# Two gated attention and feed-forward layers on one core: POOL's list re-ordered around DVE's routing, products without a reader in the filling

## What is computed

```python
x = x + tanh(g_xattn[0]) * attn0(layernorm(x), ctx)    # 16 heads of 8
x = x + tanh(g_ffn[0])   * experts(layernorm(x))       # 16 experts, best 4 of each token
x = x + tanh(g_xattn[1]) * attn1(layernorm(x), ctx)    # one head
x = x + tanh(g_ffn[1])   * butterfly_ffn(layernorm(x))

# experts
logits = xn @ wg + bg
vals, idx = top_k(logits, 4); gates = softmax(vals)    # ties: the lower index first
h = einsum('th,ehd->etd', xn, w1) + b1                 # every expert on every token
s = a * sigmoid(1.702 * a) * (b + 1)                   # a, b: even and odd columns, clipped
t = sum over e of gate_full[t, e] * (s_e @ w2_e + b2_e)

# butterfly_ffn: 9 stages on 512 columns each way, around a gelu
h = butterfly(x @ W_exp + b_exp, up_weights)
h = gelu(h + up_bias)
y = butterfly(h, down_weights) @ W_con + b_con + down_bias
```

## Time and profile before

| | us |
|---|---|
| median of 3 runs | 392.1 |
| lowest, highest | 389.17, 392.59 |
| profiled execution | 395.04 |
| its span, first to last instruction | 393.1 |

### The profile page before, as it was taken

One profiled execution on the slowest core, in us unless ns is written; L12 is line 12 of the kernel. 1 busy time (PEld: TensorE's weight loads), 2 busy tenths in 40 slices (PEclk: granted clock), 3 DMA queues, 4 the chain that ended last, 5 costly groups with the idle time before them and its releaser, 6 DMA issues.

```text
span 393.1 us, 7226 instructions
## 1 busy us (share of the span) xinstructions
PE 324.5 (83%) x2600; PEld 228.2 (58%) x2600; DVE 257.4 (65%) x602; ACT 209.6 (53%) x405; POOL 206.9 (53%) x270
## 2 busy tenths in 40 slices
PE   5758689698799912899199998799998999899986
PEld 2435567576577811666066665566655666555866
DVE  8531436556466287398868789697896887795450
ACT  2642146466366610567145584765866746855543
POOL 7463899979598999999600193002900059122120
PEclk9996759989899755699779999999999999999999
DMA  7669222645531233333133222232322433100001
GB/s 245 129 142 120 86 63 107 133 131 120 112 110 59 69 123 116 128 106 105 29 104 116 80 91 72 85 119 67 105 87 80 119 95 108 53 0 1 28 28 55
DMA packets 17235, 36.66 MB, mean 93 GB/s; under 512 B 2384, under 2 KB 4068, under 8 KB 17064
## 3 DMA queue, kind: packets, MB, share of 16 engines
q1 hardware_dynamic: 13184, 23.53, 21.2%
q0 software_dynamic: 3168, 11.54, 10.8%
q10 hardware_dynamic: 848, 1.14, 0.9%
HBM read 32.79 MB, written 1.18 MB: 86 GB/s over the span
## 4 chain that ended last, share of the span: by engine, by line
PE 36%; POOL 32%; DMA 11%; DVE 7%; issue 6%; ACT 6%; SPq 1%; ACTq 0%; DVEq 0%; POOLq 0%
PE bank L1005 9%; POOL bft L365 6%; POOL bfx L369 5%; POOL bfly L373 5%; PE bank L996 5%; PE bank L994 4%; PE bank L995 4%; DMA bw<-in_L_ffn_w 4%; DMA bw<-in_flies 4%; PE bank L1128 4%; PE bank L1113 3%; DMA x_sb<-in_x 3%; POOL bw L339 2%; POOL w_lo L388 2%; POOL v_all L422 2%
## 5 line engine op out<-in xcount | busy, mean ns | idle before, releaser
L994 PE MATMUL bank<-xhl,w_hi 128*128 128x512 f32 x128 | 76.3, 596 | 0.5 <-ACT rings L734 0.5
L734 ACT ACTIVATE rings<-bank,cols 128x512 f32<-128x512 f32 x64 | 44.1, 689 | 60.9 <-PE bank L996 50.1
L1245 DVE TENSOR_REDUCE nt<-bank 128x4 f32<-128x480 f32 x64 | 39.9, 650 | 46.2 <-PE bank L878 46.2
L1434 DVE SCALAR_TENSOR_TENSOR rings<-rings,gates 128x512 f32<-128x512 f32 x64 | 47.9, 749 | 20.9 <-ACT rings L734 20.5
L996 PE MATMUL bank<-xhl,w_hi 128*128 128x512 f32 x128 | 51.6, 403 | 0.0
L995 PE MATMUL bank<-xhl,w_lo 128*128 128x512 f32 x128 | 51.5, 402 | 0.0
L871 PE MATMUL bank<-rings,ks 32*120 32x128 f32 x512 | 41.7, 306 | 11.4 <-DMA rings<-mxr 6.2
L878 PE MATMUL bank<-ks,rings 32*128 32x120 f32 x512 | 42.9, 312 | 5.8 <-DMA rings<-qt_row 4.0
L871 PEld LDWEIGHTS bank<-rings,ks 32*120 32x120 f32 x512 | 35.2, 201 | 17.4 <-DMA rings<-mxr 8.5
L738 ACT ACTIVATE rings<-bank,b1c 128x512 f32<-128x512 f32 x64 | 44.0, 688 | 1.0 <-PE bank L996 0.6
L878 PEld LDWEIGHTS bank<-ks,rings 32*128 32x128 f32 x512 | 36.5, 213 | 6.6 <-issue 4.2
(11 more groups left out here) (227 smaller groups left out, 688.1 us busy)
## 6 DMA issues: line engine op xcount, KB each, us to landing
gates<-gate_rows SPq DMA_DIRECT2D x64, 256.0 KB, 3.1
bw<-in_flies POOLq DMA_DIRECT2D x18, 512.0 KB, 4.3
bw<-in_L_ffn_w POOLq DMA_DIRECT2D x4, 512.0 KB, 7.8
x_sb<-in_x SPq DMA_DIRECT2D x4, 256.0 KB, 8.3
x_sb<-in_L_ffn_w SPq DMA_DIRECT2D x1, 1024.0 KB, 4.9
wide<-in_ctx ACTq DMA_DIRECT2D x4, 240.0 KB, 7.2
ks<-kt_row SPq DMA_DIRECT2D x16, 60.0 KB
out<-xr SPq DMA_DIRECT2D x3, 256.0 KB, 2.4
```

What stands on the lines that cost most here:

```text
L734: act.activation(esg[:, e % 2, :], SB[1 + e % 2][:, :], ACT.Gelu_apprx_sigmoid, bias=b1_in[:, 0, e:e + 1]).then_inc(s["m_sg"], 1)
L994: pe.matmul(bk[:, :], w1_hi[:, e, branch, :], low(g), start=True, stop=False)
L1245: dve.tensor_reduce(nt[:, b % 2, OF[n], :], score_bank(b, n)[:, 0:HR * M].rearrange("p (r m) -> p r m", r=HR), AX.X, ALU.max, negate=True) ...
L1434: dve.scalar_tensor_tensor(eq[:, j, :], esg[:, j, :], GELU_LIMIT, gates[:, (n - 1) % NG, :], ALU.min, ALU.mult).then_inc(s["m_eq"], 1)
```

## The change

It has four parts.

- **POOL's list.** The seven bias stages move between the second and third split of `w1`. The 18 butterfly stages are spread: 0 to 9, `norm2(0)` and `norm_rows(0)`, 10 and 11, `remainders(0)`, then a wait until DVE has written the gates of group 0, `norm_rows(1)`, 12 and 13. In the first group of experts: the ties of group 1, a wait for its gates, `remainders(1)`, `norm2(1)`, `norm_rows(2)`, stages 14 and 15, the four `values1`. In the second group stage 16, in the third stage 17 and the bias's last stages, each behind a wait for the next group's gates.
- **DVE's list.** The routing of group 0 stands before the residual of sequence 13 as a whole; before, its first part stood ahead of it and the rest behind.
- **ACT's list.** The exponentials of the gates (L664) and the copy of the turned gates (L670) stand before the copy of the heads, not behind the copy of the turned attention.
- **PE's list.** `keep_busy` issues eight products of 128x256 whose result nobody reads, two at each of four places of the filling.

```diff
--- before.py
+++ after.py
@@ -380,7 +380,18 @@
             fetch(1)
             pool.tensor_scalar(b1c[:, :], b1_in[:, 1, :], 1.0, None, ALU.add).then_inc(s["b1_rdy"], 1)
 
+            def up_bias_rows():
+                pool.wait_ge(s["ld_ub"], 16 * 2)
+                for k in range(STAGES - 2):
+                    src, w = ubs[:, k % 2, :], ubw[:, 2 * k * P:2 * (k + 1) * P]
+                    straight(bft[0:HC, 0:P], w[:, 0:P], src)
+                    crossed(ubs[:, 2, :], w[:, P:2 * P], src, 2 ** k, P)
+                    summed(ubs[:, (k + 1) % 2, :], bft[0:HC, 0:P], ubs[:, 2, :])
+                pool.tensor_copy(ubs[:, 2, 0:1], ubs[:, 1, 0:1]).then_inc(s["us_rdy"], 1)
+
             for q in range(NQ):
+                if q == NQ // 2:
+                    up_bias_rows()
                 fetched(q)
                 src = bw[:, q % 2, :].rearrange("p (e t c) -> p e t c", e=4, t=2)
                 hi, lo = w1_hi[:, 4 * q:4 * q + 4, :, :], w1_lo[:, 4 * q:4 * q + 4, :, :]
@@ -397,14 +408,6 @@
                                    bcast[:, BO, :].unsqueeze(1).to_broadcast([P, GB, D]), ALU.add).then_inc(s["xr_rdy"], 1)
             own.then_wait(pool.tensor_tensor(bcd[:, :], bcast[:, BC, :], bcast[:, BD, :], ALU.add))
             own.then_wait(pool.tensor_scalar(bcd[:, :], bcd[:, :], tg[:, 3:4], None, ALU.mult))
-
-            pool.wait_ge(s["ld_ub"], 16 * 2)
-            for k in range(STAGES - 2):
-                src, w = ubs[:, k % 2, :], ubw[:, 2 * k * P:2 * (k + 1) * P]
-                straight(bft[0:HC, 0:P], w[:, 0:P], src)
-                crossed(ubs[:, 2, :], w[:, P:2 * P], src, 2 ** k, P)
-                summed(ubs[:, (k + 1) % 2, :], bft[0:HC, 0:P], ubs[:, 2, :])
-            pool.tensor_copy(ubs[:, 2, 0:1], ubs[:, 1, 0:1]).then_inc(s["us_rdy"], 1)
 
             def up_bias_stages():
                 pool.wait_ge(s["ub_rdy"], 1)
@@ -515,11 +518,21 @@
                 pool.tensor_tensor(rows_, rows_, bcd[:, :].unsqueeze(1).to_broadcast([P, GB, D]), ALU.add
                                    ).then_inc(s["d_bias"], 1)
 
+            def stages(ks_):
+                for k in ks_:
+                    for op in range(3):
+                        stage(k, op)
+
             def mixture(g):
                 if first(g):
                     router_ties(1)
+                    pool.wait_ge(s["m_gf"], 2)
                     remainders(1)
+                    norm2(1)
                     norm_rows(2)
+                    stages(range(STAGES + 5, STAGES + 7))
+                    for i in range(G):
+                        values1(i)
                 else:
                     rows_again(g - 1)
                     if not last(g):
@@ -527,8 +540,15 @@
                     attn1_scales(g - 1)
                     if not last(g):
                         router_ties(g + 1)
+                        pool.wait_ge(s["m_gf"], g + 2)
                     if g + 2 < G:
                         norm_rows(g + 2)
+                    if not last(g):
+                        stages((STAGES + 6 + g,))
+                    if g == G - 2:
+                        pool.tensor_copy(bft[0:1, 0:1], bfly[0:1, STAGES % 2, 0:1]).then_inc(s["bf_rdy"], 1)
+                        pool.wait_ge(s["bf_rdy"], 1)
+                        up_bias_stages()
                     if last(g):
                         pool.wait_ge(s["x3_st"], G - 2)
                         norm_scales(stats[:, 0:2 * GB, :], mean[:, 0:2 * GB], rr[:, 0:1, 0:2 * GB], 2 * GB
@@ -537,21 +557,14 @@
                         with_biases(0)
                         with_biases(1)
 
-            for k in range(2 * STAGES):
-                for op in range(3):
-                    stage(k, op)
-                if k == STAGES:
-                    norm2(0)
-                    norm_rows(0)
-                if k == 2 * STAGES - 3:
-                    remainders(0)
-                    norm_rows(1)
-            pool.tensor_copy(bft[0:1, 0:1], bfly[0:1, STAGES % 2, 0:1]).then_inc(s["bf_rdy"], 1)
-            pool.wait_ge(s["bf_rdy"], 1)
-            up_bias_stages()
-            for g in range(G):
-                values1(g)
-            norm2(1)
+            stages(range(STAGES + 1))
+            norm2(0)
+            norm_rows(0)
+            stages(range(STAGES + 1, STAGES + 3))
+            remainders(0)
+            pool.wait_ge(s["m_gf"], 1)
+            norm_rows(1)
+            stages(range(STAGES + 3, STAGES + 5))
             pipelined(pool, mixture)
             inverse_root(3, GB, False, GB)
             inverse_root(4, GB, False)
@@ -681,16 +694,16 @@
                 if b < NB:
                     exps(b, 0)
                     exps(b, 1)
+                if b == NB - 1:
+                    router_exp(0)
+                if b == NB:
+                    gates_t(0)
                 if 0 <= b - 1 < NB:
                     heads_out(b - 1)
                 if b == NB - 2:
                     normed_t(0)
-                if b == NB:
-                    gates_t(0)
                 if 0 <= b - 2:
                     attn_t(b - 2)
-                if b == NB - 1:
-                    router_exp(0)
                 if b < NB:
                     exps(b, 2)
                     exps(b, 3)
@@ -937,6 +950,12 @@
                     mm = pe.transpose((SB[0] if first(g) else PO)[0:E, u * P:(u + 1) * P], gf[:, u, :], ident[:, :])
                 mm.then_inc(s["m_g_turned"], 1)
 
+            def keep_busy(bk, n):
+
+                for _ in range(n):
+                    pe.matmul(bk[:, 0:2 * P], ident[:, :], wt[:, WK0:WK0 + 2, :].rearrange("p i c -> p (i c)"),
+                              start=True, stop=True)
+
             phase(-2, 0)
             queries(2)
             both_values(3)
@@ -950,13 +969,18 @@
             phase(-1, 0)
             pe.wait_ge(s["v_rdy"], 2 * G)
             turn_max(0)
+            keep_busy(PO, 2)
             phase(-1, 1)
             pe.wait_ge(s["kt_rdy"], G)
             pe.wait_ge(s["bo_rdy"], 1)
             for b in range(NB):
+                if b <= 1:
+                    keep_busy(PO, 2)
                 phase(b, 0)
                 if b + 1 < NB:
                     turn_max(b + 1)
+                if b == 0:
+                    keep_busy(PO, 2)
                 if b == NB - 2:
                     turn_normed(0)
                 if b >= 1:
@@ -1334,12 +1358,12 @@
                         maxima(b + 2, n)
                 if b == NB - 1:
                     router_top(0)
+                    router_ties(0)
+                    router_chosen(0)
+                    router_gates(0)
                 if b >= 2:
                     residual(b - 2)
                 if b == NB - 1:
-                    router_ties(0)
-                    router_chosen(0)
-                    router_gates(0)
                     dve.wait_ge(s["ub_turned"], 1)
                     dve.tensor_copy(ubx[:, 0, :], bank[2][:, 0:HC]).then_inc(s["ub_rdy"], 1)
 
```

## The result

| | us |
|---|---|
| before, measured beside it | 391.06 median of 4 runs (389.17 to 392.59) |
| after | 381.36 median of 4 runs (378.53 to 382.75) |
| ratio | 0.974, 95% interval 0.969 to 0.979 |
| profiled execution of after, its span | 380.01, 377.9 |

Faster by 2.6%, where 5.4% was forecast. The place to read first is the timeline of PE, and in it each group's turned gates (L937 before, L950 now). Columns: start, duration, instruction, and in brackets the idle time ahead of it.

What follows compares the result with a forecast made beforehand. It took PE's two waits for DVE's gates, 23.6 us together, as the bound, with DVE held by POOL. 15.2 + 1.4 + 10.2 - 5.5 + 0 + 0 = 21.3 us off the 392.1 median gave 370.8 us, range 362 to 380.

Steps and rivals of the forecast that it cites:

- The first term: Routing of group 0: undisturbed by POOL, PE's wait for the gates goes, 15.2 us, plus 1.4 from a faster clock.
- The second term: Routing of group 1: PE's wait of 8.3 us and the expert at half clock go, 10.2 us gained.
- The third term: Experts behind the gates of group 1: POOL's work there now comes too late or holds DVE, minus 5.5 us.
- Its first view: Second group: POOL's list brings the rows for DVE's sum 5.1 us late, stopping ACT and PE too.
- Its second view: Same stretch: 15 long POOL instructions hold DVE 16 us; spare time and cover leave a 6 us delay.
- The rest: Second and third group: stages 16 and 17 and routing without POOL's rows ready, taken as 0, between minus 3 and plus 3.
- The products: Filling: eight unread products cost 7.6 us at worst, against an earlier full clock; taken as 0, minus 5 to plus 4.
- B: Rival: stages beside experts cost more, a gain of only 12 us, 380 us; chance 0.17.
- both delays: Experts: late POOL rows and DVE held by POOL add up instead of being one delay, 12 us.
- C: Rival: DVE's small routing instructions are slow for another reason than POOL, so routing only begins earlier, 382 us; chance 0.07.
- A: Rival: POOL's list is not late in the second group, so 26.8 us are gained, 365.3 us; chance 0.17.
- D: Rival: slower, as POOL and DVE wait for each other in turn at DVE's second-group sum; chance 0.04.

Runs made afterwards that it cites:

- e4: The changed kernel without POOL's wait for the gates of group 0: ratio 0.987 to the kernel before, median 388.37 us.
- e5: The changed kernel with POOL's rows for DVE's sum made right behind `norm2(1)`, same work: ratio 0.969 to before, median 379.30 us.
- e10: e2 with the arithmetic of stages 14 and 15 left out, their transfers kept: ratio 0.948 to before, median 370.45 us.
- e9: e2 with a wait that puts stages 16 and 17 behind their group's second attention: ratio 0.965 to before, median 380.91 us.
- e1: The changed kernel without the eight products nobody reads: ratio 0.973 to before, median 382.51 us.
- e11: The kernel before with the eight products nobody reads and nothing else: ratio 1.002 to before, median 392.32 us.
- e2: The changed kernel with the four `values1` moved ahead of the low part of group 0, into the attention: ratio 0.957 to before, median 376.53 us.
- e6: The changed kernel with an always-met wait behind each of the four `values1` instructions: ratio 0.972 to before, median 380.76 us.

## Why the prediction was wrong

The sign and the two places were right, the size not: 370.8 was forecast, 381.4 came, past the upper end of 380.

**The first term, 15.2 plus 1.4.** Right. The wait went from 15.21 to 0.90 us, so 14.3 us, POOL's low part ended at 133.5, and e4 shows the mechanism.

**The second term, 10.2.** Right. Of it 8.3 us lie in front of the second gates and 1.9, the slow expert, behind them. From the first gates to the second it took 41.2 us and takes 31.3, so 9.9 us, where 8.3 and the 1.4 of the first expert were forecast; the second wait is 0.39 us, and POOL idles from 149.4 to 156.1. At the second gates the forecast comes to a lead of 24.9 us, and 26.9 was measured. That excess is luck: 2.7 us of the lead are the clock at the end of the filling.

**The third term, minus 5.5, is the step that failed.** Its first view, POOL's list too late for DVE's sum, described a delay that is not there: the rows were ready 4.5 us before DVE came, and e5 shows that making them 18 us sooner changes nothing. Its second view, DVE held by POOL beside the experts, was the true one, and was priced too low: 16 us of holding, less 6 us of spare time and 4 us of cover. The holding was sized well. In the second group of after eleven of DVE's 128x512 instructions were held, and took 17.7 us longer together than undisturbed (0.42 or 0.69 each). What failed is the 10 us taken off it. In e10 the holding in this group is 5.8 us, so 11.9 less, and the group is 11.9 us shorter (42.6 against 54.4): that part of the holding reached the end in full. Against before the group is 7.9 us longer, although the slow expert of 1.9 us is gone from it, so that the term measures minus 9.8.

Why the spare time did not cover it is my reading of the rows: POOL worked almost without a pause from 181 to 203 us and left no expert free to catch up in. One instruction was held 6.96 us, through five of POOL's, where I had read at most two; the work of three experts in hand did not cover that, PE stopped for 6.11 us, and its clock fell. Before, stages 14 and 15 had stood beside PE's wait of 15.21 us, and `values1` (170.44 to 176.70) beside experts of the first group, ahead of the wait of 8.34 us.

**The rest, 0.** The third group took 2.6 us longer than before and the last part 1.2: minus 3.8, beyond the end of minus 3. PE's waits for the exponentials in the groups of stages 16 and 17 grew by 3.4 us together. e9 brings them back to 1.3 us each and gains nothing, so which instructions the 3.8 us hang on stays open. The tail as a whole is 11.7 us longer, where 3.6 was summed (5.5 less the 1.9 of the slow expert).

**The products, 0.** Right in sum (e1, e11). The reason given, a clock that comes back earlier against 7.6 us of work, was not what decided in after: PE did get 6.7 us ahead, and the maxima's transfers took all of it.

**The median.** From profile to profile the gain is 15.2 us, from median to median 9.7. The profiled execution of before lay 4 us above its median, that of after 1.4 us below. I took the whole gain from the median. With the wait and group terms as measured (14.3 and 9.9) and the tail (minus 11.7) the sum is 12.5 us, a little more than the medians show (9.7; by the ratio's interval 8 to 12.2). Whether the re-ordered filling costs the other 2 to 3 us or it is its own variation stays open: it ended between 133.6 and 140.4 us in the profiles, and at 139.3 and 135.3 in the two with before's order.

**The rivals.** B, stages beside experts cost more, comes nearest in its mechanism, but not with "both delays", since the first is not there. Its sum was wrong: its own terms of 12, 2 and 3 us taken from 26.8 leave 9.8 us of gain, 382.3, and not 12 and 380. The upper end of the range came from that slip, and 382.3 would have held the measured 381.4. C's 382 is as near in number, and e4 and the undisturbed routing in after refute it. A is out by the tail. So is D, since the rows came in time.

## What to carry to other kernels

Taking POOL's long instructions away from a short chain of DVE that PE waits for paid in full; the same instructions then held DVE in the experts, and the holding that e10 removed had been paid in full. So ask of moved POOL work not when it is due but which DVE instructions run beside it, and whether DVE there has idle time: `values1` cost 5.5 us beside the experts and nothing measurable in the attention (e2, the best kernel here that does all the work, 4.3% under before). When an edit moves the whole program forward, measure a segment behind it as well; here it repeated within 0.2 us in five kernels while the total varied by several.

## What the runs showed of the hardware

DVE was held by POOL for far longer than one POOL instruction: 6.96 us through four `values1` instructions of 1.23 us each and the one behind them, and 6.87 us, on another instruction of DVE, through the same four and the one behind them in e5. The Trainium skill ("SBUF — State Buffer", section on two separate sides) puts the block at one whole instruction; the runs show longer ones, and the measurement decides. With a wait behind each of POOL's instructions (e6) none of DVE's beside them took over 2.33 us, and POOL's four took 6.07 us instead of 4.92. But the old `values1`, without such waits, alternated with DVE as well, in 6.26 us.

The rows of all fourteen profiles have one pattern for this. After the first 100 us, 23 DVE instructions took over 2.8 us, and each begins while POOL issues a transfer (L339), 0.3 to 0.6 us ahead of POOL's next long instruction. It ends behind the last of POOL's instructions that stand in a row without a wait for POOL's own result: two in a stage, since L373 has such a wait, five with `values1` and the one behind it. Where the row is one instruction long, the hold at the same place is 2.10 us (e2) and 2.33 us (e6). Instructions of DVE that begin while one of POOL's is running, as those beside the old `values1`, took 2.5 us at most. This is read from the rows and was not tested by an edit of its own.

And a higher clock in a stretch can be worth nothing: 1.00 instead of 0.57 from 40 to 60 us, in the profiles of after and e1, with the same time at the end. The other profiles with the products had 0.74 to 1.00 in that stretch.
